# Cross attention of a gated block: the turn of three heads back goes to the head of each step on TensorE

## The reference

```python
# x: 32 batches x 100 queries x 256; ctx: 32 x 361 x 256; 16 heads of 16
Q = layernorm(x) @ Wq.T + bq ; K = ctx @ Wk.T + bk ; V = ctx @ Wv.T + bv
scores = einsum('bhqd,bhkd->bhqk', Qm, Km) / sqrt(16)    # 100 x 361 per head
scores = where(mask, scores, finfo.min)
A = einsum('bhqk,bhkd->bhqd', softmax(scores), Vm)
x = x + tanh(g_xattn) * (A @ Wo.T + bo)
```

## Time and profile before

| | |
|---|---|
| median of 3 runs | 1936.9 us (1934.24 to 1937.22) |
| profiled execution, its own time | 1935.28 us |
| its span | 1933.5 us |
| mean granted TensorE clock | 0.995 of full speed |
| TensorE, VectorE, ScalarE, GpSimd busy | 97%, 78%, 59%, 48% of the span |

### The profile page before, as it was taken

One profiled execution on the slowest core, in us unless ns is written; L12 is line 12 of the kernel. 1 busy time (PEld: TensorE's weight loads), 2 busy tenths in 40 slices (PEclk: granted clock), 3 DMA queues, 4 the chain that ended last, 5 costly groups with the idle time before them and its releaser, 6 DMA issues. The chain is left out here.

```text
span 1933.5 us, 57514 instructions
## 1 busy us (share of the span) xinstructions
PE 1873.0 (97%) x13454; PEld 1145.7 (59%) x13454; DVE 1503.0 (78%) x4285; ACT 1137.4 (59%) x3588; POOL 935.6 (48%) x1368
## 2 busy tenths in 40 slices
PE   5999999999997999999999999999999999999998
PEld 2678888888875555444444445545555555555553
DVE  6688888899887962555555556668999999999989
ACT  3678888888886444444444445545555555555543
POOL 4122222222212011666666666665776676776767
PEclk9999999999998999999999999999999999999999
DMA  3777888888871585000000023122222222222201
GB/s 124 144 117 118 119 120 120 119 119 120 119 98 55 214 330 208 27 27 20 21 27 27 27 67 105 55 66 72 71 80 66 80 74 70 80 67 79 75 13 66
DMA packets 192148, 174.22 MB, mean 90 GB/s; under 512 B 51921, under 2 KB 183378, under 8 KB 190034
## 3 DMA queue, kind: packets, MB, share of 16 engines
q1 hardware_dynamic: 189906, 165.06, 37.7%
q0 software_dynamic: 2176, 8.39, 1.2%
HBM read 112.41 MB, written 60.98 MB: 90 GB/s over the span
## 5 line engine op out<-in xcount | busy, mean ns | idle before, releaser
L1475 POOL TENSOR_TENSOR o_side<-o_side,o_tmp 128x256 f32 (+1 forms) x528 | 397.8, 753 | 194.7 <-POOL o_side L1475 72.3
L1244 PE MATMUL e_pv<-e_vw,e_xhi 128*128 (+1 forms) x1600 | 475.9, 379 | 1.2 <-ACT e_out L1167 1.2
L1177 ACT ACTIVATE big<-e_pv,gates 128x128 f32<-128x128 f32 x800 | 228.4, 369 | 280.2 <-PE e_pv L1244 278.6
L1603 ACT ACTIVATE o_tmp<-o_py,gates 128x256 f32<-128x256 f32 x528 | 222.4, 475 | 192.0 <-PE o_py L1675 138.6
L640 ACT ACTIVATE c_ex<-c_sm,c_nmax 100x361 f32<-100x361 f32 x512 | 302.6, 593 | 54.7 <-DVE c_nmax L523 49.7
L1675 PE MATMUL o_py<-o_whi,a_chi 128*128 128x512 f16 x800 | 304.3, 380 | 0.1
L1675 PE MATMUL o_py<-o_whi,a_clo 128*128 128x512 f16 x800 | 303.8, 380 | 0.0
L1675 PE MATMUL o_py<-o_wlo,a_chi 128*128 128x512 f16 x800 | 303.6, 379 | 0.0
L1244 PE MATMUL e_pv<-e_vw,e_xlo 128*128 (+1 forms) x800 | 303.2, 379 | 0.0
L523 DVE CUSTOM_DVE_ANT_0 c_sm<-c_ps,c_mbias 100x361 f32<-100x361 f32 x512 | 268.3, 525 | 38.9 <-PE c_ps L725 32.7
L1110 DVE TENSOR_SCALAR e_acc<-e_pv,gates 128x128 f32<-128x128 f32 x400 | 121.7, 346 | 218.6 <-PE e_pv L1244 218.5
(11 more groups left out here) (165 smaller groups left out, 3218.8 us busy)
## 6 DMA issues: line engine op xcount, KB each, us to landing
qk<-e_out SPq DMA_DIRECT2D x16, 1600.0 KB, 5.2
c_kst<-k_parts SPq DMA_DIRECT2D x256, 90.2 KB, 4.9
a_q<-qk SPq DMA_DIRECT2D x64, 200.0 KB, 2.4
a_k<-qk SPq DMA_DIRECT2D x64, 200.0 KB, 2.4
v<-e_out SPq DMA_DIRECT2D x20, 640.0 KB, 3.3
a_v<-v SPq DMA_DIRECT2D x64, 200.0 KB
c_ctx<-in_ctx_t SPq DMA_DIRECT2D x32, 361.0 KB, 3.4
e_wst<-in_v_w POOLq DMA_DIRECT2D x8, 1024.0 KB, 8.2
```

The source lines that it names most:

```text
L1177: act.activation(tmp[:, hh, e, :], p_v[:, hh, 1, e * PD:(e + 1) * PD], ACT.Copy, scale=gate).then_inc(s_av, 1)
L1244: last = pe.matmul(p_v[:, hh, half, :], a[:, c, bass.ds(t * P, P)], vw[:, bass.ds(col + (w * DC + c) * VW, 512)], start=j == 0, stop=j == ...
L1475: pool.tensor_tensor(side[:, x.t, :], side[:, x.t, :], tmp[:, slot(x, r), j, :], ALU.add).then_inc(s_pool, 1)
L1603: act.activation(tmp[:, slot(x, r), j, :], p_y[:, q, j, :], ACT.Copy, scale=gate).then_inc(s_av, 1)
```

## The change

In TensorE's step loop of the cross attention the two lagging calls move. Before, a step issued the scores of head i, the projections of that step, the turn of head i-3 and the value matmuls; after, it issues the turn of head i-3, the scores of head i, the value matmuls, and the projections. Nothing else in the program differs.

```diff
             def body(b):
                 for i in range(XH):
+                    lagging(b, i, LAG_T, turn)
                     scores(b, i)
+                    lagging(b, i, LAG_A, attend)
                     if i in ahead and later(b, ahead[i][0]):
                         n, work, *args = ahead[i]
                         work(later(b, n), *args)
                     if i in behind and not is_first(b):
                         work, *args = behind[i]
                         work(b.before(), *args)
-                    lagging(b, i, LAG_T, turn)
-                    lagging(b, i, LAG_A, attend)
```

## The result

The changed kernel took 1986.9 us (median of 4 runs, 1980.6 to 1991.9) beside 1937.1 for the kernel before (4 runs, 1934.2 to 1941.3): a ratio of 1.0255, 95% interval 1.0236 to 1.0274. It is slower by 50 us where 35 were forecast, inside the range of 1957 to 1990. The profiled execution took 1991.1 us (span 1989.3, granted clock 0.988), 55.8 more than the profiled one of before. The four runs differ with the mean granted clock: the two at 0.993 took 1981 and 1983 us, those at 0.986 and 0.988 took 1992 and 1991.

The account below looks back on a forecast made before the run. No engine alone was the bound: three near 90% busy hand heads to one another. Period 17.33 against 16.19 us, +1.14 over 31 periods, 35.3 us, gave 1972 us; own range 1957 to 1990, wider range 1945 to 1990.

Parts of the forecast that it names:

- The mechanism: Cross attention: a turn waiting for the copy two heads back holds up scores behind it, leaving VectorE without work; +1.14 us a batch.
- The turn of head 14: Step 1: largest single term, one chain of 3.83 us from scores of head 14 to scores of head 1.
- The list: One cross-attention batch walked in the new order until it repeated: period 17.33 us against 16.19, with the waiting turns marked.
- the pieces of a batch: TensorE's work in one cross-attention batch, summed to 14.65 us against a period of 16.1 to 16.2.
- the value matmuls' seam: Four steps a batch: value matmuls directly behind scores, with 0.15 us taken for the scores.
- Over the 31 periods: Cross attention from first to last batch: each period 1.14 us longer, 35.3 us in all; stages behind only start later.
- That earlier turns take waits away: Faster rival: earlier turns in cross attention end other engines' waits for turned blocks; 1915, or 1933 with VectorE's part alone; chance 0.08.
- The slack of 1.5 us: No-change rival: TensorE's spare time in each cross-attention batch swallows the moved stall; 1937 us; chance 0.06.
- The half case: Rival: earlier copies let VectorE run ahead, leaving 0.3 to 0.6 us a batch; 1947 to 1956 us; chance 0.12.
- The Trainium skill's rule on weight loads: TensorE's turns: loads pulled ahead of matmuls in flight would be covered, giving the lower sum, 1959 us; the forecast kept 0.40.

Follow-up runs that it names:

- The edit that shortens its chain: Against the changed kernel, both low parts of the next keys made in step 0 behind its masked pass: 1976.4 us, ratio 1.0198.
- the two mixed kernels: Changed order with the old order in steps 0, 1, 3, 7, 8, 13, 14: 1953.4 us; the complement, changed order only in those seven: 1965.2 us.
- The version that beat both kernels: Against the kernel with scores, value matmuls, projections, turn: second high part of the next keys made ahead of head 13's copy; 1929.4 us, ratio 0.9952.

## Why the prediction came out as it did

**The mechanism held.** A turn that waits for the copy two heads back stands in front of scores whose own inputs are there. The run with the scores ahead of the turn, all else as in the change, is level with the kernel before; that shows the place. The waits show the kind: 72.3 us of turns' loads for VectorE's copies, VectorE's wait for scores at 60.4 (60 was named), busy 83% (83% named), no wait of scores' loads for the row maxima, and waits for turned blocks of at most 1.0 us for VectorE and 0.7 for ScalarE in the whole program. The turn of head 14 is the longest stall: its interval is 1.83 us where 1.30 would do. The edit that shortens its chain gave back 10 us.

**The list held, to 0.06 us in 14 of 16 intervals.** The two that didn't, from heads 4 and 8, are 0.10 longer each. With 0.06 and 0.03 more in the stalled intervals from heads 2 and 0, and small differences in the others, they make the 0.31 by which the period, 17.64, is above 17.33. Two slips in the working change nothing in the sum: the pieces of a batch add up to 14.67 us, not 14.65, and from copy to turn the rows have 0.52 where the list takes 0.51.

**The first term that was mis-sized** is the value matmuls' seam: the sum took 0.15 us from scores to the value matmuls behind them, the spacing of scores to any other work. The trace has 0.25 (307.37 to 307.62 above), and then 0.65 and 0.39, near the 0.65 and 0.40 that were taken. It shows in the two steps where nothing else is late, 0.20 us a batch or 6 us in 31; in the two others the turn behind the value matmuls waits anyway. With the smaller differences it is 0.31 a batch, 9.6 us in 31.

**The second** is that all batches were priced alike. "Over the 31 periods" covers the steady state. The first batch was 3.8 us longer, 2.4 more than the 1.41 of a middle one, and the last, which isn't a period between scores and was left at nothing, 7.0. In parts of both, TensorE's instructions ran at half speed. 35.3 + 9.6 + 2.4 + 7.0 makes 54.3; with 2.3 in the stages behind and 0.5 before the stage it is 57.1, beside 55.8 in the profiles, since the middle batches grew by 1.41 and not by 1.14 + 0.31. The median of the runs, 50 us over, has less of the low clock, and the two runs at 0.993 are 44 and 46 over, about what the steady batches alone give. The run with the old order in the outer batches came out 9 us lower and had the clock up in the whole stage.

The other profiles say how much of this second term is the order. In six of the 14 the clock fell in the first batch, and three of those have the scores ahead of the turn. With such a fall the first batch took 16.9 to 19.5 us, without one 15.6 to 17.1, and the kernel before, at 15.6, is the shortest of all. The stages behind vary between 1336.5 and 1339.9 us with no relation to the order, so the 2.3 lie within their scatter. From the scores that begin the last batch to the end of the stage, the two kernels with the turn first in all steps and the old lags took 28.7 and 29.4 us, with 17 us of them at the lower level; the others took 20.7 to 24.6. That part goes with the changed order, but no profile has this order there with the clock up.

**The rivals.** That earlier turns take waits away was not wrong in itself: with the turn second, ScalarE's waits for turned blocks went from 17.0 to 3.2 us, but it was worth nothing that can be measured. The slack of 1.5 us didn't swallow the stalls. The half case, 10 to 19 us, fell too.

**The Trainium skill's rule on weight loads** (the Trainium skill, TensorE: Matmul & The Clock Gate, Step-by-step: what each phase is for), that they are pulled ahead of matmuls in flight, would have given 1959 as the prediction used it. The Trainium skill says it for loads whose row groups are free or that go to a spare weight buffer, and no row shows whether that is so here. In the trace no such gain shows for turns behind a wait (0.40 us, not 0.30, from 304.21 to 304.61), nor at the seams of the value matmuls. That matmuls keep program order, as the same section of the Trainium skill says, agrees with the stalled scores: they started 0.40 behind the turn at 304.21, though their own inputs had long been there.

**What stays open** is how the loss divides between the turns that wait in the list and the others; the two mixed kernels gave 29 and 18 us, with waits of their own. How much of the outer batches' 10.8 us is the order and how much the low clock is open too: half-speed rows stand in both batches, but what made the clock fall isn't shown, and chance between runs isn't excluded.

## What to carry to other kernels

On an engine that works in order, put first what waits for nothing, and behind it what waits for a buffer: the same two calls cost nothing in one order and 50 us in the other. Price a new order by walking one period with the spacings of the trace until it repeats, with every engine's queue in it; here that gave the intervals to 0.10 us or better. Price the first and the last period by themselves. If shifting a lag only turns the wait round (turn for copy, copy for turn), look instead for one instruction that is queued behind a wait it doesn't need; moving the keys' high part was worth some 24 us in one kernel (ratio 1.0082 to 0.9952).

## What the runs showed of the hardware that was not expected

The granted clock fell inside the cross attention of the changed kernel, from 75.6 to 82.4 us in its first batch and from 621.7 to 638.8 in its last. In the profile of before it first falls at 593.7, when only the output projection of the last batch is left. In the last batch of the changed kernel the rows ran like this, the first two at the lower level, the last two where it ends:

```profile
634.09 0.93 PE L732 MATMUL c_pt<-ident,c_ex 100*121 100x100 f32 x3
634.81 0.51 PE L725 MATMUL c_ps<-c_kst,c_qst 128*100 128x361 f16 x1
...
638.57 0.57 PE L732 MATMUL c_pt<-ident,c_ex 100*121 100x100 f32 x3
638.98 0.32 PE L725 MATMUL c_ps<-c_kst,c_qst 128*100 128x361 f16 x1
```

From a turn to its scores it takes 0.72 us there and 0.41 when the clock is back. Over 630 to 650 us, of which the first 8.8 are at the lower level, TensorE was busy 79% of the time and the granted clock was 0.78:

```profile
630.00:650.00 20.00, 15.84 (x153) 11.62 (x152) 11.12 (x40) 9.66 (x29) 0.00 (x0) 0.78 0.02 6
```

The same happened in the first batch, where turns took 0.57 to 0.72 us until their scores between 75.7 and 82.3 us. TensorE had been idle there for 1.17 and 1.38 us just before. These gaps alone don't tell when the clock falls. The two kernels with VectorE's copies one head earlier have the same two in their first batch, and their clock stayed up. The kernel before and the two with the value matmuls moved up and the old lags have gaps of 1.16 and 0.89 us; its clock stayed up, theirs fell at 75.4 and 76.1 us. The version that beat both kernels is one of those two.
